# Extra TensorE products in the waits of a two-layer attention and expert kernel

## The reference

```python
# 1: channel attention: q, k, v = h @ qkv_w.T + qkv_b for 4 batches of 1024 rows
w = softmax(einsum('ncq,nck->nqk', q, k * scale), axis=2)   # 128 x 128 per batch
a = einsum('nqk,nck->ncq', w, v); out = a @ proj_w.T + proj_b + x
# 2: ternary feed-forward, 128 -> 512 -> 128, rms-normalised, gelu between
# 3: attention over 1024 tokens, 16 heads of dimension 8, with rope
# 4: top-2 experts, 24 experts, 4 groups of 1024 tokens, capacity 86 each
h = moe_apply(x, combine, dispatch, W1, b1)      # 128 -> 512
h = relu(layer_norm(h, ln_hid_w[g], ln_hid_b[g]))
out = moe_apply(h, combine, dispatch, W2, b2)    # 512 -> 128, then layer_norm(out + x)
```

## Time and profile before

| | us |
|---|---|
| median of 3 runs | 1117.26 |
| lowest, highest run | 1112.72, 1119.31 |
| the profiled execution | 1115.23 |
| its span, first to last instruction | 1113.4 |

### The profile page before, as it was taken

The page is one execution under the profiler, slowest core; times in us unless marked ns, Lnnn a source line. Parts: engine busy times, 40 slices in busy tenths (PEclk is TensorE's granted clock), DMA queues, the critical chain, the costliest instruction groups (busy, mean ns, idle before and its releaser), DMA issues. The chain is left out here.

```text
span 1113.4 us, 19273 instructions
## 1 busy us (share of the span) xinstructions
PE 896.5 (81%) x6642; PEld 419.9 (38%) x6642; DVE 603.1 (54%) x2008; ACT 761.4 (68%) x1092; POOL 350.1 (31%) x332
## 2 busy tenths in 40 slices
PE   2866983775699999999989999998988988786650
PEld 2653653332122222222222222332355667355650
DVE  7379857887201545454443416252561346488877
ACT  1234342356799999999999999998575684655520
POOL 5412523455300000000000000030677667774553
PEclk9676986888799999999999999999988999888885
DMA  5000000246344412111121211136797775666451
GB/s 170 1 1 0 1 1 0 59 113 171 87 150 147 117 44 62 44 57 45 30 57 44 64 43 49 38 92 171 223 204 153 180 238 147 215 206 181 142 138 54
DMA packets 92539, 109.68 MB, mean 99 GB/s; under 512 B 12125, under 2 KB 66014, under 8 KB 92330
## 3 DMA queue, kind: packets, MB, share of 16 engines
q1 hardware_dynamic: 78932, 78.80, 23.4%
q0 software_dynamic: 11264, 27.80, 10.7%
q10 hardware_dynamic: 2262, 2.06, 0.6%
HBM read 68.90 MB, written 39.71 MB: 98 GB/s over the span
## 5 line engine op out<-in xcount | busy, mean ns | idle before, releaser
L1517 ACT ACTIVATE s_e<-s_ps 128x1024 f32<-128x1024 f32 x512 | 476.7, 1069 | 12.2 <-PE s_ps L1687 11.3
L1700 PE MATMUL s_acc<-s_e,s_v 128*32 128x512 f32 x2048 | 274.1, 608 | 0.7 <-ACT s_e L1517 0.7
L1135 POOL DMA_INDIRECT x_in<-x_tokens,rows_of x72 | 72.1, 1001 | 459.5 <-DVE rows_of L1291 424.1
L1687 PE MATMUL s_ps<-qk 51*128 51x512 bf16 x1024 | 180.2, 387 | 23.4 <-ACT s_e L1517 10.2
L1687 PEld LDWEIGHTS s_ps<-qk 51*128 51x128 bf16 x1024 | 41.3, 93 | 273.0 <-ACT s_e L1517 254.4
L2036 PE MATMUL e_py<-w,qk 128*96 128x128 f32 x768 | 102.9, 282 | 0.0
L2036 PEld LDWEIGHTS e_py<-w,qk 128*96 128x96 f32 x768 | 92.6, 170 | 0.0
L2006 PE MATMUL e_ph<-w,qk 128*32 128x512 f32 x576 | 80.3, 632 | 6.2 <-ACT e_hs L2099 6.2
L2131 ACT ACTIVATE qk<-e_pn,ln_hid 128x384 f32<-128x384 f32 x96 | 63.0, 664 | 31.4 <-PE e_pn L2020 31.4
L1135 POOL DMA_INDIRECT e_ya<-y_rows,take x64 | 66.3, 1036 | 30.8 <-issue 26.6
L1700 PEld LDWEIGHTS s_acc<-s_e,s_v 128*32 128x32 f32 x2048 | 40.4, 108 | 80.3 <-issue 52.9
(11 more groups left out here) (429 smaller groups left out, 1448.9 us busy)
## 6 DMA issues: line engine op xcount, KB each, us to landing
h_rows<-e_hs SPq DMA_DIRECT2D x54, 256.0 KB, 4.4
w<-in_w SPq DMA_DIRECT2D x10, 768.0 KB, 5.7
qk<-parts_q SPq DMA_DIRECT2D x60, 96.0 KB
qk<-parts_k SPq DMA_DIRECT2D x60, 96.0 KB
h_rows<-x_res SPq DMA_DIRECT2D x16, 256.0 KB, 4.2
qk<-parts_k SPq DMA_DIRECT2D x60, 64.0 KB
parts_q<-b_parts SPq DMA_DIRECT2D x16, 192.0 KB, 2.7
parts_k<-b_parts SPq DMA_DIRECT2D x16, 192.0 KB, 2.7
```

The source lines that it names most:

```text
L1135: nc.gpsimd.indirect_dma_start(dst, None, rows, bass.IndirectOffsetOnAxis(ap=idx, axis=0), compute_op=op).then_inc(R["landed"][k % FLIGHT] ...
L1517: nc.scalar.activation(E[g % 4][:, 2 * pair:2 * pair + 2, :], pS[BUFFER["score", 2 * g + pair]][:].rearrange("p (a s) -> p a s", a=2), ACT ...
L1687: last = nc.tensor.matmul(pS[BUFFER["score", 2 * g + pair]][:, a * CH:(a + 1) * CH], K[c % 2][rows, pair, j * P:(j + 1) * P], Q[c % 2][row ...
L1700: last = nc.tensor.matmul(acc[hu % 2][32 * h:32 * h + 32, :], V4[c % 2][:, j, h, :], E[g % 4][:, h, :], start=j == 0, stop=j == TB - 1)
```

## The change

Ten matrix products are added whose results nothing reads. One stands behind the last L552 product and ahead of the wait for `r_done`, with no wait of its own. Nine stand in groups of three at blocks m = 6, 12 and 18, ahead of their first transposes; each group first waits for `rows_done` to reach 4 and for the first add of a partner to block m. All ten are f32, with 128 x 128 weights and 512 columns.

```diff
             s_wk.then_inc(r_mm, 1)
+            mm(pO[1][:], wqs[:], ZT[:, 0:CH], start=True, stop=True)
             pe.wait_ge(r_done, 2)
...
                 if m % NB == 0:
+                    if m:
+                        pe.wait_ge(R["rows_done"], GR)
+                        pe.wait_ge(add_done, TPB * (m - NB) + 1)
+                        for i in range(3):
+                            mm(pM[:], ident[:], W1[:, i, :], start=True, stop=True)
                     for c in range(FC):
                         h_transposes(m, c)
```

## The result

| | before | changed |
|---|---|---|
| median of 20 runs, us | 1117.27 | 1112.53 |
| lowest, highest run | 1112.72, 1122.56 | 1110.29, 1117.71 |
| span of the profiled execution | 1113.4 | 1112.2 |

The ratio is 0.996, with a 95% interval of 0.9946 to 0.9974: 4.5 us faster, between 2.9 and 6.0. The forecast was 1112.

The account below looks back on a forecast made before the run. PE at half clock in the first attention's scores was taken as what everything behind waits for. Terms -4.2 + 0 + 0 + 0 from a mean of 1116.1 gave 1111.9, rounded to 1112 us; range 1109 to 1115, over all 1107.5 to 1118.5.

Parts of the forecast that it names:

- The product is hidden: Ahead of the first attention's scores: the added product ends under DVE's second copy, with 0.5 us to spare.
- The pause lost the clock, and filling it keeps it through the scores, -4.2 us: First attention: filling most of PE's 1.36 us pause keeps full clock for all 16 score products, -4.2 us.
- Rival 1: First attention's scores: the clock falls anyway, perhaps from single-row products; nothing gained, 1116 us; chance 0.25 with both its forms.
- its form with a fall in the middle: First attention: the clock falls partway through the scores, about 1114 us; shares the chance of 0.25.
- It passes on: Behind the last score: DVE's work and `m(0)` move with it, `m(0)` to 49.5 from 53.70; half clock stays behind.
- its first part: The product ahead of the first attention's scores: -4.2 us, bounds -5.2 and +0.4.
- Blocks 6 and 12 give the clock and nothing at the end: Expert stage: fillers keep full clock behind both heads, 0 us at the end; bounds -1.1 and -0.3, each to +0.1.
- The sign that DVE's wait for partners grows by what PE gained: Expert stage, before block 11: DVE's 8.17 us wait for partners should lengthen by PE's gain.
- the bound of 1.1 us of gain: Block 6 of the expert stage: the most its three products could gain, 1.1 us, against 0 expected.
- rival 2: Expert stage: PE's gain there reaches the end, 2.2 us more, 1109.8 us; chance 0.15.
- Block 18 stays at half clock: Block 18's head: 4.7 us of pause stay empty, transposes at half clock as before; 0 us, bounds -0.8 and 0.
- Rival 3, slower: Heads of blocks 6 and 12: the products delay real work, 2.7 us twice; 1122 us, chance 0.10.

Follow-up runs that it names:

- the heads alone, third set: Only the nine products at blocks 6, 12 and 18 added to the kernel before, run again on another chip: 1116.17 us, ratio 0.9997.

## Why the prediction was right, step by step

- *The product is hidden.* Right: 1.12 us in the pause, PE goes on when DVE is done, at 0.31 us of wait.
- *The pause lost the clock, and filling it keeps it through the scores, -4.2 us.* This is the step that was mis-sized, and half of its reason fell. The clock went over the pause in all six profiles with the product and single-row products, and fell 3.7 to 5.2 us into the scores, after nine to twelve products. Without the product it went over the pause too, in all four profiles, and fell after two products in three of them and after four in one, less than 2 us into the scores. The scores took 7.7 to 8.9 us with it and 10.4 to 10.9 without, 2.0 to 3.2 us in place of 4.2. With the products at 128 rows the same pause costs no clock in the scores. Rival 1 named this ("if it is these that lose the clock"), and its form with a fall in the middle, 1114, is what PE's timeline shows.
- *It passes on.* Right: L573 came 3.58 us behind the scores before and after, and the kernel with the product alone kept 3.2 us (1.2 to 5.2). But by the signs that the prediction names its first part is wrong: the scores do not take 6.7 us, L573 starts at 50.53 and not near 49.5, and the feed-forward starts 2.9 us earlier (86.96, before 89.81), of which only 1.7 lie behind the first score, and not 4.
- *From 2.7 us in the scores to 4.5 us in the median.* In part open. The interval reaches down to 2.9. From the first product of the scores to the first exponential of the second attention the profiles have 247.1, 246.6 and 245.8 us without the product (before, heads alone twice) and 243.7, 241.6, 241.7 and 242.0 with it, 4.2 us apart in the mean, of which some 1.6 us arise behind the first attention, in a stretch that nothing was changed in. There the trace shows the clock again. These are the 15 us that begin 165 us behind the first transposes of the feed-forward, before and with the product alone:

```profile
254.81:269.81 15.00, 13.52 (x39) 7.03 (x39) 11.70 (x14) 10.65 (x19) 8.27 (x7) 0.77 0.59 159
252.15:267.15 15.00, 12.78 (x40) 6.30 (x40) 12.61 (x16) 12.32 (x22) 10.12 (x8) 0.89 0.62 168
```

The clock falls at the same place in both and stays at 0.50 for some 7 us in the first and some 3.5 in the second, which is worth up to 1.7 us, and the exponential comes 2.2 us earlier behind the feed-forward's start. All four of the profiles named that have the product show 0.89 there. But of the three without it one has 0.89 too (the heads alone, third set), so this is no sure work of the product: how often the clock comes back early there with it and without is open.
- *Blocks 6 and 12 give the clock and nothing at the end.* Right as far as it can be measured: 0.48 us left of the pause, 1.00 behind it, and partners that come no earlier; 0.9997 (0.9978 to 1.0016) for the heads alone. The sign that DVE's wait for partners grows by what PE gained is not clear: 8.50 us in the changed kernel and 8.10 with the heads alone, before 8.17. The interval of +-2.1 us excludes neither the bound of 1.1 us of gain nor rival 2 (2.2 us). The expert stage speaks against them, with 247.7 and 245.5 us with the heads against 247.4 and 245.9 without, but the zero rows' 252.0 show how much it varies.
- *Block 18 stays at half clock.* Right: 5.12 us without a product are left (4.7 were reckoned), then six transposes in 1.54 us, as before.
- *Rival 3, slower.* Did not come: both heads were reached at full clock.
- *The rule of the Trainium skill* (page "TensorE: Matmul & The Clock Gate", section "Part 1: The HAM clock gate (the "warmup" mystery)"), that the moment of a change varies from run to run: the place of the fall did, from the tenth to the thirteenth of the same products with the filler and from the third to the fifth without it. That the pause did or did not lose the clock from run to run, no profile shows.

The total came right with luck. The term for the scores was 1.5 us too large (4.2 against 2.7 in the mean of the profiles), because the clock fell again within them, which the prediction had as a form of its rival 1; some 1.6 us that it had only as a bound of 1 us, a clock that comes back at another place, made it up in the profiles. Whether they do so in the medians stays open.

## What to carry to other kernels

Before filling a pause to keep TensorE's clock, look at what stands on both sides of it: here the clock was lost where products with one row of weights stood behind the pause, and padding them with rows of zeros gave in one edit about as much as the whole change (4.2 us, between 2.3 and 6.1), with full clock and half the time between starts. Filling paid where the work behind the pause is PE's own (the stretch behind the scores: 3.3 us of its stage where the filler fitted the wait, 1.1 where it overran it) and gave nothing that could be measured where the next wait is for a gather (blocks 6 and 12), though the clock was kept there. A filler costs nothing only as long as it is shorter than the wait at both clocks; three products of 512 columns took 2.74 us at full clock and 4.76 us where most of it ran at half.

## What the runs showed of the hardware that was not expected

- Products of 128 columns in f32 that alternate between 128 rows and one row of weights start 0.415 us apart at full clock; with 128 rows throughout, 0.22 us. So a product with one row is not cheap: a pair of the two kinds takes 0.83 us, a pair of full ones 0.44.
- The granted clock fell in the middle of such products while PE was busy for all of 3.60 us before it (window 38.10 to 41.70 of the changed kernel). A busy PE in the profile is no sure sign that the clock holds.
- Rows of zeros kept the clock as data did: the scores of the kernel with zero rows ran at 1.00 from 38.21 to their end at 42.45, as those of the kernel with repeated rows of data did for the same 4.2 us.
- The same program took 1117 us on one chip and 1172 us on another. In the kernel with the product alone 51.4 of the 55.0 us between the two spans lie in the expert stage: from block 0's first transposes to the last `down` 297.3 us on the one, 245.9 us on the other. What made it slower there is not shown.
